# Longer Prelu chains, GpSimd in the making of weights, and the maximum of a kernel taken by TensorE

## What is computed

```
xn = layernorm(x)
K  = real(ifft(roots of the DPLR kernel))        # 512 values
y  = causal convolution of xn's rows with K + D * xn
W  = NF4_CODE[q] * absmax                        # gate, up: 1792 x 512; down: 512 x 1792
h  = silu(xn Wg^T) * (xn Wu^T)
out = x + y + h Wd^T
```

## Time and profile before

| | us |
|---|---|
| median of 3 runs | 467.42 (466.54 to 467.91) |
| the profiled execution | 466.52 |
| its span, first to last instruction | 464.7 |
| PE busy | 446.5 (96%) |
| DVE busy | 400.2 (86%) |
| ACT busy | 284.9 (61%) |
| POOL busy | 61.5 (13%) |

### The profile page before, as it was taken

One profiled execution on the slowest core, in us unless ns is written; L12 is line 12 of the kernel. 1 busy time (PEld: TensorE's weight loads), 2 busy tenths in 40 slices (PEclk: granted clock), 3 DMA queues, 4 the chain that ended last, 5 costly groups with the idle time before them and its releaser, 6 DMA issues.

```text
span 464.7 us, 7186 instructions
## 1 busy us (share of the span) xinstructions
PE 446.5 (96%) x2595; PEld 253.9 (55%) x2595; DVE 400.2 (86%) x658; ACT 284.9 (61%) x480; POOL 61.5 (13%) x116
## 2 busy tenths in 40 slices
PE   0699999999999999999999999999999999999997
PEld 0554444444444444444444444466544688888886
DVE  4899689979798887988999888876799899999993
ACT  7966565587597965769777696794132543545340
POOL 0464499400000000000001000023100000000000
PEclk9999999999999999999999999999999999999999
DMA  8482545122425234112132225256570021101111
GB/s 273 86 284 80 114 88 147 47 70 67 159 69 181 95 132 158 59 56 86 51 95 71 91 41 158 78 183 209 169 292 0 1 92 47 44 3 47 47 47 45
DMA packets 31830, 47.20 MB, mean 102 GB/s; under 512 B 13044, under 2 KB 14132, under 8 KB 31284
## 3 DMA queue, kind: packets, MB, share of 16 engines
q1 hardware_dynamic: 30516, 42.56, 30.0%
q0 software_dynamic: 1280, 4.20, 2.8%
HBM read 35.93 MB, written 8.72 MB: 96 GB/s over the span
## 4 chain that ended last, share of the span: by engine, by line
PE 90%; DVE 3%; POOL 2%; ACT 2%; DMA 1%; issue 1%; SPq 0%; POOLq 0%
PE bank L1875 34%; PE bank L2006 21%; PE bank L2108 21%; PE bank L2059 8%; PE bank L2049 6%; DMA work<-in_q_up 1%; POOL h L718 1%; PE bank L1910 1%; ACT h L816 0%; DVE h L1174 0%; DVE h L1337 0%; PE bank L1965 0%; DVE bank L1281 0%; DVE work L1167 0%; DVE work L1163 0%
## 5 line engine op out<-in xcount | busy, mean ns | idle before, releaser
L1875 PE MATMUL bank<-xT,w 128*128 128x512 f16 (+1 forms) x732 | 164.9, 378 | 1.9 <-DVE w L1174 1.7
L1875 PEld LDWEIGHTS bank<-xT,w 128*128 128x128 f16 x732 | 71.9, 99 | 86.5 <-DVE w L1174 2.1
L816 ACT ACTIVATE work<-work 128x512 f32<-128x512 int32 x136 | 77.8, 623 | 5.0 <-DVE work L1146 2.5
L2108 PE MATMUL bank<-wd,work 128*128 128x256 f16 x504 | 56.2, 273 | 0.0
L2108 PEld LDWEIGHTS bank<-wd,work 128*128 128x128 f16 (+1 forms) x504 | 49.3, 98 | 6.0
L2006 PE MATMUL bank<-h 128*128 128x512 f16 x198 | 48.1, 379 | 0.0
L1106 ACT ACTIVATE work<-h 128x896 f16<-128x896 f32 x30 | 27.9, 942 | 27.8 <-DVE h L1783 18.3
L2108 PE MATMUL bank<-h,work 128*128 128x256 f16 x378 | 42.2, 273 | 0.0
L2108 PEld LDWEIGHTS bank<-h,work 128*128 128x128 f16 x378 | 37.0, 98 | 4.3
L900 ACT ACTIVATE work<-bank,sc 128x512 f32<-128x512 f32 x45 | 30.4, 678 | 13.2 <-PE bank L1875 12.9
L2059 PE MATMUL bank<-wd,h 128*128 128x512 f16 x168 | 36.4, 379 | 0.0
(11 more groups left out here) (183 smaller groups left out, 643.3 us busy)
## 6 DMA issues: line engine op xcount, KB each, us to landing
h<-in_x SPq DMA_DIRECT2D x8, 512.0 KB, 6.2
moved<-h SPq DMA_DIRECT2D x4, 1024.0 KB, 4.7
xT<-in_x POOLq DMA_DIRECT2D x16, 256.0 KB, 3.4
h<-moved SPq DMA_DIRECT2D x4, 1024.0 KB, 10.5
out<-xT SPq DMA_DIRECT2D x15, 256.0 KB, 2.1
work<-in_q_gate SPq DMA_DIRECT2D x14, 256.0 KB, 2.7
work<-in_q_up SPq DMA_DIRECT2D x14, 256.0 KB, 2.9
work<-in_am_gate SPq DMA_DIRECT2D x28, 128.0 KB, 3.0
```

What stands on the lines that cost most here:

```text
L816: nc.scalar.activation(knee_of(u, k), qs[:, u % 2, :], KNEE, scale=scale, bias=bias, alpha=below).then_inc(knee_done, 1)
L1875: mm = nc.tensor.matmul(out_b, weights(k)[:, unit, wl, f, :], xT[:, TPC * c + first:TPC * c + last, xl, f, :], start=(i == 0), stop=(i == ...
L2108: mm = nc.tensor.matmul(out_b, part, w, start=(n == 0), stop=(n == 3 * KT - 1))
```

## The change

There are three parts.

1. **Chains from unit 11 on.** `CHAINED` grows from the last 4 units to 31. The right chain loses one pass: its former first two become a maximum and a subtraction made by POOL (`first_pass`), which writes the room from which ACT's r0 reads. So a unit has six ACT passes, l0, r0, l1, r1, l2, r2. DVE's RIGHT and LEFT steps and ACT's clamp go for 27 units. DVE takes WHOLE of a unit, then the low half of the one before, then SCALED. The whole unit goes to one of three rooms in turn.
2. **Halves by POOL.** For units 11 to 37 (`POOL_HALVES`) POOL writes the high half (`weight_hi`) and, for gate units, the scaled whole copy (`gate_copy`). ACT does it for the others.
3. **The maximum by PE.** PE transposes krow (`kernel_max`), DVE reduces the 128 values and works out the powers on one partition, and PE sends two numbers to all partitions by a product with a row of ones (`kernel_scale`). The last small stages move into window 13. The ones get a tile of their own.

The core of the diff:

```diff
+RIGHT_FROM = 7.021753311157227
 RIGHT_CHAIN = [
-    (0.2770431637763977, -1.945328712463379, 0.0),
-    (1.0, -0.7235357761383057, 0.886136531829834),
+    (0.2770431637763977, -0.7235357761383057, 0.886136531829834),
     (1.0, -0.554499626159668, 0.7530558705329895),
...
-CHAIN_ORDER = ("r0", "l0", "r1", "l1", "r2", "l2", "r3")
+CHAIN_ORDER = ("l0", "r0", "l1", "r1", "l2", "r2")
...
-CHAINED = range(UNITS - 4, UNITS)
+CHAINED = range(11, UNITS)
+POOL_HALVES = range(CHAINED[0], UNITS - 4)
...
+        def room_read(u):
+
+            return dq_after(u - 1, LEFT) if u == CHAINED[0] else dq_after(u - 2, WHOLE)
...
-                if u >= 2:
-                    sp.wait_ge(knee_done, PASSES_AT[u - 2] + (2 if u - 2 in CHAINED else KNEES))
+                if u - 2 in CHAINED:
+                    sp.wait_ge(first_done, u - 2 - CHAINED[0] + 1)
+                    sp.wait_ge(knee_done, PASSES_AT[u - 2] + 1)
+                elif u >= 2:
+                    sp.wait_ge(knee_done, PASSES_AT[u - 2] + KNEES)
...
+            def first_pass(u):
+
+                pool.wait_ge(q_ld[u % 2], 16 * (u // 2 + 1))
+                pool.wait_ge(dq_done, room_read(u))
+                pool.tensor_scalar(chain_room(u, "r"), qs[:, u % 2, :], RIGHT_FROM, RIGHT_FROM,
+                                   ALU.max, ALU.subtract).then_inc(first_done, 1)
+
+            def weight_hi(u):
+
+                pool.wait_ge(dq_done, dq_after(u, SCALED))
+                unit = SEQ[u]
+                if unit < GU:
+                    before = room_before(unit // 2)
+                    if unit % 2 and before in BLOCKED:
+                        pool.wait_ge(m_done, m_at(before, 4))
                     else:
-                        row = turns[:, a, c:c + 3 * a + 1:a]
-                    pool.tensor_copy(turned[:, c, a, :], row).then_inc(turn_done, 1)
-            pool.wait_ge(t_done, 3)
-            pool.partition_all_reduce(kmax, krow, P, bass.bass_isa.ReduceOp.max).then_inc(kmax_done, 1)
+                        pool.wait_ge((gate_done, up_done)[unit % 2], WHOLE_COUNT[LAST_USE[before]])
+                pool.tensor_scalar(weight_of(u)[HI], whole_of(u), scale_of(u), None, ALU.mult).then_inc(phi_done, 1)
+
+            def gate_copy(u):
+
+                if SEQ[u] >= GU or SEQ[u] % 2:
+                    return
+                pool.wait_ge(dq_done, dq_after(u, SCALED))
+                pool.wait_ge(w_done, 4 * blocked(SEQ[u] // 2))
+                pool.tensor_scalar(sums_room(SEQ[u] // 2)[0], whole_of(u), scale_of(u), None, ALU.mult).then_inc(g_done, 1)
+
+            pool.wait_ge(v_done, V_STEPS)
+            first_pass(CHAINED[0])
+            for u in POOL_HALVES:
+                first_pass(u + 1)
+                weight_hi(u)
+                gate_copy(u)
+                if u == made_before(NM - 3) - 1:
+                    turned_rows()
+            first_pass(UNITS - 3)
+            first_pass(UNITS - 2)
 
             for t in range(NT):
                 pool.wait_ge(conv_done, t + 1)
                 pool.dma_start(res[:, t, :], x_v[:, t, :]).then_inc(xr_ld[t], 16)
+                if t == 3:
+                    first_pass(UNITS - 1)
...
-                if i == 0:
+                if i:
+                    act.wait_ge(knee_done, PASSES_AT[u] + CHAIN_ORDER.index(f"{side}{i - 1}") + 1)
+                elif side == "r":
+                    act.wait_ge(first_done, u - CHAINED[0] + 1)
+                else:
                     act.wait_ge(q_ld[u % 2], 16 * (u // 2 + 1))
-                    if u - 1 in CHAINED:
-                        act.wait_ge(dq_done, dq_after(u - 2, WHOLE))
-                    else:
-                        act.wait_ge(dq_done, dq_after(u - 1, LEFT))
-                else:
-                    act.wait_ge(knee_done, PASSES_AT[u] + CHAIN_ORDER.index(f"{side}{i - 1}") + 1)
+                    act.wait_ge(dq_done, room_read(u))
                 scale, bias, below = (RIGHT_CHAIN if side == "r" else LEFT_CHAIN)[i]
-                nc.scalar.activation(room, room if i else qs[:, u % 2, :], KNEE, scale=scale, bias=bias,
...
                     if p == ACT_AT[u]:
-                        weight_hi(u - 1)
+                        if u - 1 in ACT_HALVES:
+                            weight_hi(u - 1)
+                        gate_copy(u - 1)
...
-                        dve.wait_ge(wlo_done, u - 1 if u < 4 else u)
-                    before = SEQ[u - 1] if u else GU
+                        dve.wait_ge(wlo_done, u - 1 if u < 4 or u in CHAINED else u)
+                    past = u - 1
+                    if u in CHAINED:
+                        past = u - 3 if u - 3 >= CHAINED[0] - 1 else None
+                    before = GU if past is None or past < 0 else SEQ[past]
...
-                dve.wait_ge(whi_done, u + 1)
+                if u in POOL_HALVES:
+                    dve.wait_ge(phi_done, u - POOL_HALVES[0] + 1)
+                else:
+                    dve.wait_ge(whi_done, ACT_HALVES.index(u) + 1)
...
-                        i += 2
+                        i = (3, 2, 4)[i]
...
-                    dve.wait_ge(kmax_done, 1)
+                    dve.wait_ge(km_tp, 1)
+                    small(v.tensor_reduce, kmax, bank[7][0:1, 0:P], AX.X, ALU.max)
                     for i in range(3):
                         exponent(i, kmax, kpow, kinv)
-                    small(v.tensor_scalar, s_k, kinv, 2.0 ** 13, None, ALU.mult)
-                    small(v.tensor_scalar, c_conv, kpow, 2.0 ** -14 / XS, None, ALU.mult)
+                elif s == 4:
+                    dve.wait_ge(km_bc, 1)
+                    small(v.tensor_scalar, s_k, bank[7][:, P + 1:P + 2], 2.0 ** 13, None, ALU.mult)
+                    small(v.tensor_scalar, c_conv, bank[7][:, P:P + 1], 2.0 ** -14 / XS, None, ALU.mult)
                 else:
...
             def toeplitz_stage(slot):
-                if slot >= 6:
-                    toeplitz(slot - 4)
+                if slot == 6:
+                    toeplitz(2)
 
             def kernel_stage(slot):
-                if slot == 1:
+                if slot == 2:
+                    toeplitz(3)
+                elif slot == 4:
                     toeplitz(4)
+                elif slot == 5:
+                    toeplitz(5)
...
+            def kernel_max():
+
+                pe.wait_ge(t_done, 3)
+                nc.tensor.transpose(bank[7][0:1, 0:P], krow, ident[:]).then_inc(km_tp, 1)
+
+            def kernel_scale():
+
+                pe.wait_ge(sc_done, KMAX_MADE)
+                nc.tensor.matmul(bank[7][:, P:P + 2], ones[0:1, :], sc[0:1, 17:19], start=True, stop=True).then_inc(km_bc, 1)
...
                 blocked_product(k, 1)
+                if k == NM - 1:
+                    kernel_max()
                 products(n, (1,))
                 blocked_product(k, 5)
                 if k == NM - 4:
                     s4_sums()
                 blocked_product(k, 2)
                 blocked_product(k, 6)
+                if k == NM - 1:
+                    kernel_scale()
```

54 lines of the change are left out of this document (35 added, 19 removed).

## The result

The changed kernel takes 473.31 us (median of 4 runs, 471.61 to 473.78) against 467.09 before (4 runs): a ratio of 1.0125, with a 95% interval of 1.0095 to 1.0156. It is slower by 6.2 us, and above the upper end of the forecast range. Its profiled execution took 473.78 us with a span of 472.0, which is 7.3 us over the one before.

The account below looks back on a forecast made before the run. PE was taken to set the time from about 48 us on; 0.5 us for two added operations plus a 1.0 us stall in window 11 gave 1.5, hence 468.9 us on the median (8 in 10: 467.2 to 472.0).

Parts of the forecast that it names:

- First pass 0.77: done at s = 252.0: Window 11: unit 30's first pass on POOL takes 0.77 us, ends at 252.0, and PE stands 1.0 us at product 3.
- the bound of 2.7 us on the stall: Window 11, upper bound: dearer slips, copies behind SCALED and a 1.59 us first pass put s at 253.7, stall 2.7 us.
- No PE wait elsewhere behind 48 us: Sign expected in the profile after: beyond about 1 us in window 11, PE waits nowhere after 48 us.
- the change touches nothing there but the place of the ones: Start before 48 us: the change alters only where the ones lie, so no gain is seen; from the faster rival, chance 0.04.
- was on no path: The removed all-reduce on POOL and a copy on ACT were on no path; no time was entered for them.
- 0.5 us for the two fp32 operations: Window 13 on PE: the added transpose and two-column product cost 0.25 + 0.25 = 0.5 us, bounds 0.4 and 0.8.
- nothing for DVE's 23 us: DVE loses two steps in each of 27 units, 32 us, all beside PE: worth 0.
- nearly nothing for ACT and the halves: ACT keeps six instructions per chained unit, worth 0; POOL as a whole keeps up with its 66 added instructions.
- the maximum covered in window 13: Window 13: DVE's small steps for the maximum end near 293.1, PE asks at 294.6, so covered by 1.5 us.
- nothing at the tail: Tail: POOL's DMAs of x run up to 1.7 us late but catch up before PE needs the banks; worth 0.
- POOL is too slow for every window: Rival, chance 0.10: in three-unit windows first passes come 0.3 us late, window 11 adds 1.5 more; 471.9 us.
- The port costs more: Rival, chance 0.13: each slip costs DVE a whole POOL instruction, 0.75 us; window 11 stalls 1.9 us; 469.8 us.

Follow-up runs that it names:

- e5: Changed kernel with GpSimd's first passes written in five forms, high halves in three, gate copies in two, to measure prices (weights come out wrong): 470.24 us, 1 run.
- e14: Changed kernel with each first pass on GpSimd written as multiply and add instead of max and subtract (weights come out wrong): 470.98 us, ratio 1.0077 to before.
- e10: Changed kernel with high halves and gate copies on GpSimd written as multiply and add zero instead of multiply alone: 472.72 us, ratio 1.0118 to before.
- e2: Changed kernel with chains, first passes and high halves on GpSimd starting at unit 12 instead of unit 11: 473.91 us, ratio 1.0140 to before.
- e6: Kernel before with only the tile of ones given a place of its own: 467.02 us against 466.98, ratio 1.0001.
- e4: Kernel before with only the kernel's maximum made by TensorE and the ones in their own tile, chains and halves as before: 468.12 us, ratio 1.0030.
- e13: Changed kernel with an all-reduce, its result unused, put back as GpSimd's last operation: 471.70 us, ratio 1.0102 to before.
- e15: Changed kernel with turned-row copies behind unit 30's first pass, chains from unit 12, halves and gate copies adding zero, unused all-reduce last: 467.92 us, ratio 1.0020 to before.
- e3: Changed kernel with the maximum still made by GpSimd's all-reduce, behind unit 34's high half, without the two TensorE operations: 485.18 us, ratio 1.0390 to before.
- e9: Changed kernel with GpSimd waiting for VectorE's seventh step of the first rstd ahead of the ident's affine_select: 472.84 us, ratio 1.0123 to before.
- e12: Changed kernel with turned-row copies behind unit 30's first pass, chains from unit 12, halves and gate copies adding zero, ident held back: 470.16 us, ratio 1.0059 to before.
- e11: Changed kernel with high halves and gate copies back on ScalarE, first passes staying on GpSimd: 472.82 us, ratio 1.0120 to before.

## Why the prediction was wrong

**The failed step is the price of the first pass on GpSimd**, "First pass 0.77: done at s = 252.0". The row of 768 ns was of a multiply and add; the first pass is a max and subtract and takes 1.93 us (e5). The text named the int32 input as what had no row, did not ask about the pair of operations, and took the row for its idle DVE. Its upper bound, 1.59, was too low for the same reason; the bound of 2.7 us on the stall does cover the 2.14, but by copies later than they were, so that is luck. Set in the frame of before (3.95 us off), the rest of that chain came out as worked: copies from 249.63 (forecast 249.7) to 251.16 (251.2), first pass done at 253.18 (252.0), product 3 at 5.10 behind it (5.1), stall 2.14 (1.0). The 1.1 is the price. e14 gives the price back and gets 0.8; its 470.98 us lie inside the forecast range. The high halves and gate copies were mispriced in the same way (1.57 for 0.77), and POOL is busy 182.7 us where 90 to 130 were forecast, but that was off the path (e10).

**"No PE wait elsewhere behind 48 us" failed by the same price.** Window 4 was not looked at: of the waits, I followed the one behind the copies, and asked of the others only whether three units fit a window. The first chained unit is another case, since its room comes free late (DVE's left step of unit 10) and a silu is queued behind it. It cost 1.2 us; e14 leaves 0.4 of it, e2 none at that product.

**"the change touches nothing there but the place of the ones" is a second failed step, with a cause of its own.** I read the start in instructions, and their order is indeed the same. The ones are innocent (e6). The loss came with the removed all-reduce (e4), and e13 brings the old chain back. The term that I had put at nothing with "was on no path" shows at the other end of the program: without an all-reduce at its end a kernel starts window 3 later by 0.7 to 1.2 us in the profiles at full clock and by up to 2.8 in those where the clock falls, against 0.3, 0.3 and 1.1 in those with one (e6, e15, e13). Shown: with an all-reduce last, POOL stands 9 to 10 us ahead of affine_select and the chain takes 7.65 us; with none, or with one in mid-program (e3), neither. That the execution before leaves POOL in another configuration, which is then loaded again behind MODIFY_POOL_CONFIG, fits all of this, e3's 7.5 us too, but it is argued: the gap itself has no row. Why two of the small operations then take 0.59 and 0.20 us and not 1.20 and 1.41 stays open: up to the first of them DVE's instructions lie at the same distance in both, to 0.02 us, and holding the ident back to 10.4 us without an all-reduce changes nothing (e9).

**Right:** PE as the bound; 0.5 us for the two fp32 operations (0.50, e4); nothing for DVE's 23 us (e12 and e15 have no wait above 0.2 us behind 40 us and gain nothing); nearly nothing for ACT and the halves (0.6 and 0.5 us, e10 and e11); the maximum covered in window 13 (no wait for sc_done); nothing at the tail (from the convolution to the end the difference stays 7.26 us).

**The rivals.** Nearest in time was "POOL is too slow for every window", 471.9, but its mechanism did not occur: windows 5 to 10 and 12 show no wait. "The port costs more" gave the right size in window 11 (1.9) by a wrong cause, as u_done came when forecast. The sum of the first counts five windows of three units beside window 11; there are six, which would have made it 472.2.

**The sum as measured**, for the profiled execution: start 2.6, of it some 1.7 by the clock; window 4 1.2; window 11 2.1; the two operations 0.5; a wait of 0.36 in window 13; 0.5 not placed: 7.3 us. The wait of 0.36 is in this profile alone: e2, e9 and e13 have window 11's 2.1 us in full and no wait in window 13, so it does not follow from it, and its cause stays open.
